# A three-layer graph attention kernel on one core: 806 columns instead of 808, and the node stage in four overlapped parts

## What is computed

```python
def _egat_layer(nf, ef, src, dst, W_ni, W_nj, W_fij, W_node, attn, bias):
    f_ni = nf @ W_ni
    f_nj = nf @ W_nj
    f_fij = ef @ W_fij
    f_out = f_ni[src] + f_nj[dst] + f_fij + bias
    f_out = jax.nn.leaky_relu(f_out, 0.2).reshape(-1, H, D)
    e = jnp.einsum('ehd,hd->eh', f_out, attn)
    emax = jax.ops.segment_max(e, dst, num_segments=N)
    a = jnp.exp(e - emax[dst])
    denom = jax.ops.segment_sum(a, dst, num_segments=N)
    a = a / denom[dst]
    h = (nf @ W_node).reshape(-1, H, D)
    m = h[src] * a[:, :, None]
    h_out = jax.ops.segment_sum(m, dst, num_segments=N)
    return (h_out, f_out)
...
h = jnp.maximum(_layernorm(x, axis=-1), 0.0)
for l in range(NL):
    nfh, efh = _egat_layer(nf, ef, src, dst, W_ni[l], W_nj[l], W_fij[l], W_node[l], attn[l], bias[l])
    nf = nfh.mean(axis=1)
    ef = efh.mean(axis=1)
return x + nf
```

## Time and profile before

| what | value |
|---|---|
| median of three runs | 3382.18 us |
| the profiled execution | 3382.53 us |
| its span, first to last instruction | 3380.7 us |
| PE busy | 2677.5 us, 79% |
| DVE busy | 2183.4 us, 65% |
| ACT busy | 1648.5 us, 49% |
| POOL busy | 2459.0 us, 73% |
| moved by DMA | 346.73 MB, mean 103 GB/s |

### The profile page before, as it was taken

The page is one execution under the profiler, slowest core; times in us unless marked ns, Lnnn a source line. Parts: engine busy times, 40 slices in busy tenths (PEclk is TensorE's granted clock), DMA queues, the critical chain, the costliest instruction groups (busy, mean ns, idle before and its releaser), DMA issues.

```text
span 3380.7 us, 34349 instructions
## 1 busy us (share of the span) xinstructions
PE 2677.5 (79%) x8858; PEld 1997.1 (59%) x8858; DVE 2183.4 (65%) x5325; ACT 1648.5 (49%) x3374; POOL 2459.0 (73%) x2595
## 2 busy tenths in 40 slices
PE   2299988888887288888888988827888888888883
PEld 1177766666665256666666666625666666666663
DVE  5288876767676247667676766624766767676663
ACT  0166655555555045555555555513555555555541
POOL 5777777777775777777777777667777777777773
PEclk8655555555555555555555555555555555555555
DMA  6143433333322323333323233232233232322222
GB/s 226 50 132 108 138 107 112 103 117 104 117 80 105 97 74 108 110 107 107 123 95 122 95 107 101 84 102 83 85 102 100 85 104 95 103 90 85 87 75 80
DMA packets 131212, 346.73 MB, mean 103 GB/s; under 512 B 48232, under 2 KB 88682, under 8 KB 111444
## 3 DMA queue, kind: packets, MB, share of 16 engines
q1 hardware_dynamic: 45492, 282.83, 22.3%
q0 software_dynamic: 82688, 46.77, 8.7%
q10 hardware_dynamic: 2838, 14.94, 1.1%
HBM read 131.12 MB, written 213.25 MB: 102 GB/s over the span
## 4 chain that ended last, share of the span: by engine, by line
POOL 51%; PE 19%; issue 18%; DMA 7%; DVE 4%; ACT 1%; POOLq 0%; DVEq 0%; ACTq 0%
POOL rows L453 49%; PE f_ps L567 7%; PE f_ps L575 7%; DMA rows<-nf_tab,src_sb 5%; PE xT_ps L557 4%; POOL edge_first L464 2%; DVE U L1070 1%; DMA U<-fix_tab 1%; POOL z L507 1%; DVE lr L1004 1%; DVE U L906 1%; PE wide_ps L639 1%; ACT f_low L686 0%; ACT up L731 0%; PE xT_ps L627 0%
## 5 line engine op out<-in xcount | busy, mean ns | idle before, releaser
L453 POOL DMA_INDIRECT rows<-nf_tab,src_sb x2424 | 2288.3, 944 | 761.6 <-issue 728.7
L575 PEld LDWEIGHTS f_ps<-w_out,lr 128*128 128x128 f32 x4848 | 1167.5, 331 | 622.4 <-issue 577.7
L567 PE MATMUL f_ps<-xT,w_edge 97*128 97x512 f32 x1212 | 1157.3, 1057 | 10.4 <-ACT xT L678 10.4
L557 PE MATMUL xT_ps<-ident,rows 128*97 128x128 f32 x2424 | 692.0, 439 | 502.2 <-DMA rows<-nf_tab,src_sb 352.1
L575 PE MATMUL f_ps<-w_out,lr 128*128 128x36 f32 (+1 forms) x4848 | 1052.8, 371 | 17.9 <-DVE lr L1004 17.8
L1004 DVE TENSOR_TENSOR lr<-f_ps,f_low 128x512 f32<-128x512 f32 x606 | 416.3, 687 | 890.5 <-ACT f_low L686 886.5
L557 PEld LDWEIGHTS xT_ps<-ident,rows 128*97 128x97 f32 x2424 | 518.2, 279 | 558.4 <-DMA rows<-nf_tab,src_sb 350.0
L1070 DVE TENSOR_TENSOR_SCAN U<-wide_ps,U 128x272 f32<-128x272 f32 (+1 forms) x1224 | 797.9, 715 | 1.2 <-ACT wide_ps L720 0.7
L678 ACT ACTIVATE xT<-xT_ps 97x512 f32<-97x512 f32 x606 | 357.7, 590 | 396.0 <-PE xT_ps L557 390.8
L686 ACT ACTIVATE f_low<-f_ps 128x512 f32<-128x512 f32 x606 | 360.6, 595 | 336.4 <-PE f_ps L567 334.7
L720 ACT ACTIVATE wide_ps<-e_dec 128x289 f32<-128x289 f32 (+1 forms) x612 | 403.4, 676 | 161.8 <-DVE U L1070 158.9
(11 more groups left out here) (135 smaller groups left out, 615.5 us busy)
## 6 DMA issues: line engine op xcount, KB each, us to landing
u_tab<-up SPq DMA_DIRECT2D x150, 1088.0 KB, 4.2
rows<-nf_tab,src_sb POOLq DMA_INDIRECT x2424, 2.4
first_st<-edge_first SPq DMA_DIRECT2D x48, 768.0 KB, 6.0
ef_tab<-ef_new SPq DMA_DIRECT2D x32, 768.0 KB, 4.2
ef_st<-ef_tab SPq DMA_DIRECT2D x32, 768.0 KB
edge_first<-first_st ACTq DMA_DIRECT2D x16, 768.0 KB, 12.1
ef_st<-in_edge_attr_dram SPq DMA_DIRECT2D x16, 672.0 KB
U<-fix_tab SPq DMA_DIRECT2D x3, 1062.5 KB
```

The costliest lines, as they stand in the source:

```text
L453: eng.indirect_dma_start(rows[q % RING][:, c * K:c * K + D], None, nf_tab[:, :], bass.IndirectOffsetOnAxis(ap=src_sb[:, t:t + 1], axis=0)) ...
L557: mm = eng.transpose(xT_ps[y][0:K, u * P:(u + 1) * P], rows3[q % RING][:, a * GT + u, :], ident[:, :])
L567: eng.matmul(f_ps[n % 3][:, :], w_edge[l][:, :], xT[y][0:K, :], start=True, stop=True).then_inc(f_ready, 1)
L575: mm = eng.matmul(f_ps[n % 3][:, u * m:(u + 1) * m], lr[y][:, u * P:(u + 1) * P], w_out[l][:, 0:m], start=True, stop=True)
```

## The change

T is computed as the number of columns that the edges need, 806, instead of whole groups of four, 808; the last group of a layer has two columns, and transposes, copies, leaky step and scores are as wide as the group. The wait for gathered rows counts the real columns. The last block has 6 columns, the last super block 38.

The nodes form four parts of 8, 8, 4 and 5 columns. Part a's result lies in a PSUM bank of its own: the two banks of `wide_ps`, `f_ps[0]` and `f_ps[1]`. DVE prepares a part (lines 1185 to 1198) and takes the result of the part ahead of it after that, in `take_nodes`. In the last layer `take_nodes` adds the result to x itself, and SP stores the output in four pieces. Each wait and index that depends on the parts follows.

```diff
--- before.py
+++ after.py
@@ -36,8 +36,8 @@
     C = D + 1
     K = C + 2 * D
     DST0, EF0 = C, C + D
-    NG = -(-E // (P * GT))
-    T = NG * GT
+    T = -(-E // P)
+    NG = -(-T // GT)
     NS = -(-T // SUP)
     NB = -(-T // SB)
     GB = SB // GT
@@ -58,6 +58,9 @@
 
     def sub_w(b):
         return min(SB, T - b * SB)
+
+    def grp_w(g):
+        return min(GT, T - g * GT)
 
     def groups_to(q):
         l, s = divmod(q, NS)
@@ -161,7 +164,7 @@
         wide_ps = ps("wide_ps", [P, 2 * GT * P])
         dbc = [wide_ps[:, y * GT * P:(y + 1) * GT * P] for y in range(2)]
         wts = dbc[0][:, (C - D // 2) * W1:(C - D // 2) * W1 + H * SB]
-        n_ps = wide_ps[0:NQ, 0:NCOL * D]
+        n_ps = [a[0:NQ, :] for a in (dbc[0], dbc[1], f_ps[0], f_ps[1])]
         runs_ps = ps("runs_ps", [P, GT * P])
         same_b = [runs_ps[:, s * SUP:(s + 1) * SUP] for s in range(2)]
         cut_b = [runs_ps[:, (2 + s) * SUP:(3 + s) * SUP] for s in range(2)]
@@ -246,7 +249,7 @@
         fix_clear = sem("fix_clear")
         fix_in = [sem(f"fix_in{a}") for a in range(2)]
         marked = sem("marked")
-        z_in = [sem(f"z_in{a}") for a in range(3)]
+        z_in = [sem(f"z_in{a}") for a in range(4)]
         nd = sem("nd")
         s_turned = sem("s_turned")
         sT_ready = sem("sT_ready")
@@ -254,14 +257,13 @@
         x_out = sem("x_out")
 
         groups = [range(g, min(g + GT, NCOL)) for g in range(0, NCOL, GT)]
-        parts = [range(0, 2), range(2, 4), range(4, len(groups))]
+        parts = [range(0, 2), range(2, 4), range(4, 5), range(5, len(groups))]
         part_cols = [range(groups[p[0]][0], groups[p[-1]][-1] + 1) for p in parts]
         col_part = [a for a, cols in enumerate(part_cols) for _ in cols]
         NPART = len(parts)
-        assert part_cols[2][0] * D == GT * P
         JS, NDS = 11, 4 * NPART
         fix_cols = [range(0, part_cols[2][0]), range(part_cols[2][0], NCOL)]
-        part_fix = [0, 0, 1]
+        part_fix = [0, 0, 1, 1]
         FIXW = SUP * D
         DB = NQ
         DSTEP = -(-D // (GS - 3))
@@ -278,8 +280,9 @@
         def ef_in_count(q):
             return 16 * sum(ef_loads(a) for a in range(q % 2, q + 1, 2))
 
-        def visits(q, a):
-            return sum((v % NS) * GS + a < NG for v in range(q % RING, q + 1, RING))
+        def rows_sem_to(q, a):
+            return 16 * sum(grp_w((v % NS) * GS + a) for v in range(q % RING, q + 1, RING)
+                            if (v % NS) * GS + a < NG)
 
         def carry_of(u, w):
             return u[:, 0:CH * (w + 1)].rearrange("p (c t h) -> p c t h", t=w + 1, h=H)
@@ -416,10 +419,12 @@
                         eng.wait_ge(nf_ready, (l + 2) * NPART)
                         store_nf()
 
-                eng.wait_ge(nf_ready, (L + 1) * NPART + 1)
-                eng.dma_start(out.rearrange("(q b) d -> q (b d)", b=NCOL), x_sb[:, :]
-                              ).then_inc(x_out, 16)
-                eng.wait_ge(x_out, 16)
+                for a, cols in enumerate(part_cols):
+                    c = slice(cols[0] * D, (cols[-1] + 1) * D)
+                    eng.wait_ge(nf_ready, L * NPART + (a + 1))
+                    eng.dma_start(out.rearrange("(q b) d -> q (b d)", b=NCOL)[:, c], x_sb[:, c]
+                                  ).then_inc(x_out, 16)
+                eng.wait_ge(x_out, 16 * NPART)
 
             @block.gpsimd
             def _(eng):
@@ -518,8 +523,8 @@
                                            u_end[:, :], None,
                                            bounds_check=N - 1, oob_is_err=False
                                            ).then_inc(u_fixed, 16)
-                    gather_z(1)
-                    gather_z(2)
+                    for a in range(1, NPART):
+                        gather_z(a)
 
             @block.tensor
             def _(eng):
@@ -548,12 +553,12 @@
                         if a == 0:
                             eng.wait_ge(dst_spread, (q + 1) * D)
                             eng.wait_ge(ef_put, q + 1)
-                        eng.wait_ge(src_rows[q % RING][a], visits(q, a) * 16 * GT)
+                        eng.wait_ge(src_rows[q % RING][a], rows_sem_to(q, a))
                         if n >= 2:
                             eng.wait_ge(xT_ready, n - 1)
                         else:
                             eng.wait_ge(counted, NCOL)
-                        for u in range(GT):
+                        for u in range(grp_w(g)):
                             mm = eng.transpose(xT_ps[y][0:K, u * P:(u + 1) * P],
                                                rows3[q % RING][:, a * GT + u, :], ident[:, :])
                         mm.then_inc(turned, 1)
@@ -564,14 +569,15 @@
                         if n >= 3:
                             eng.wait_ge(sc_ready, n - 2)
                             eng.wait_ge(ef_ready, min(n - 2, (L - 1) * NG))
-                        eng.matmul(f_ps[n % 3][:, :], w_edge[l][:, :], xT[y][0:K, :],
+                        eng.matmul(f_ps[n % 3][:, 0:grp_w(g) * P], w_edge[l][:, :],
+                                   xT[y][0:K, 0:grp_w(g) * P],
                                    start=True, stop=True).then_inc(f_ready, 1)
 
                     def scores(g):
                         n, y = n0 + g, (n0 + g) % 2
                         eng.wait_ge(lr_ready, n + 1)
                         m = M if l < L - 1 else H
-                        for u in range(GT):
+                        for u in range(grp_w(g)):
                             mm = eng.matmul(f_ps[n % 3][:, u * m:(u + 1) * m],
                                             lr[y][:, u * P:(u + 1) * P], w_out[l][:, 0:m],
                                             start=True, stop=True)
@@ -636,7 +642,8 @@
                             node_turn(n + 1)
                         eng.wait_ge(sT_ready, l * len(groups) + (n + 1))
                         for u, b in enumerate(groups[n]):
-                            mm = eng.matmul(n_ps[:, b * D:(b + 1) * D],
+                            a, c = col_part[b], b - part_cols[col_part[b]][0]
+                            mm = eng.matmul(n_ps[a][:, c * D:(c + 1) * D],
                                             xT[n % 2][:, u * DB:(u + 1) * DB],
                                             w_mean[:, l * D:(l + 1) * D],
                                             start=True, stop=True)
@@ -675,7 +682,8 @@
                         eng.wait_ge(turned, n + 1)
                         if n >= 2:
                             eng.wait_ge(f_ready, n - 1)
-                        eng.activation(xT[y][0:K, :], xT_ps[y][0:K, :], ACT.Copy
+                        w = grp_w(g) * P
+                        eng.activation(xT[y][0:K, 0:w], xT_ps[y][0:K, 0:w], ACT.Copy
                                        ).then_inc(xT_ready, 1)
 
                     def lower(g):
@@ -683,7 +691,8 @@
                         eng.wait_ge(f_ready, n + 1)
                         if n >= 2:
                             eng.wait_ge(lr_ready, n - 1)
-                        eng.activation(f_low[y], f_ps[n % 3][:, :], ACT.Copy, scale=SLOPE
+                        w = grp_w(g) * P
+                        eng.activation(f_low[y][:, 0:w], f_ps[n % 3][:, 0:w], ACT.Copy, scale=SLOPE
                                        ).then_inc(f_low_ready, 1)
 
                     def take_scores(g):
@@ -694,14 +703,15 @@
                         if i == 0 and k >= 2:
                             eng.wait_ge(prod_done, k - 1)
                         eng.wait_ge(o_ready, n + 1)
-                        o3 = f_ps[n % 3][:, 0:GT * m].rearrange("p (t m) -> p t m", m=m)
-                        eng.activation(sc3[k % 2][:, i * GT:(i + 1) * GT, :], o3[:, :, 0:H],
+                        w = grp_w(g)
+                        o3 = f_ps[n % 3][:, 0:w * m].rearrange("p (t m) -> p t m", m=m)
+                        eng.activation(sc3[k % 2][:, i * GT:i * GT + w, :], o3[:, :, 0:H],
                                        ACT.Copy).then_inc(sc_ready, 1)
                         if l < L - 1:
                             if a == 0 and q >= 2:
                                 eng.wait_ge(ef_out[q % 2], ef_stores_to(q - 2))
                             c = ((q % 2) * SUP + a * GT) * D
-                            eng.activation(ef_new[:, c:c + GT * D]
+                            eng.activation(ef_new[:, c:c + w * D]
                                            .rearrange("p (t d) -> p t d", d=D),
                                            o3[:, :, H:M], ACT.Copy).then_inc(ef_ready, 1)
 
@@ -1001,7 +1011,8 @@
                         eng.wait_ge(f_low_ready, n + 1)
                         if n >= 2:
                             eng.wait_ge(o_ready, n - 1)
-                        eng.tensor_tensor(lr[y], f_ps[n % 3][:, :], f_low[y], ALU.max
+                        w = grp_w(g) * P
+                        eng.tensor_tensor(lr[y][:, 0:w], f_ps[n % 3][:, 0:w], f_low[y][:, 0:w], ALU.max
```

(24 more changed lines are left out.)

## The result

The changed kernel takes 3362.67 us, the median of six runs from 3361.76 to 3363.67, beside 3382.21 us for the kernel before, the median of six as well (3381.65 to 3383.82): a ratio of 0.9942, interval 0.9929 to 0.9954, or 19.5 us less. The forecast was 3370.3 us, with a range from 3365.5 to 3374.8. The sign was right, and the gain is larger than forecast by 7.6 us and lies outside the range.

A forecast was written before the change was run, and what follows sets the result against it. GpSimd's row gathers were taken as the bound, with slack at each layer's end. Width 3.9, layer changes 0.6, node stage 6.8, store 0.5 and start-up 0.05 sum to 11.9 us: 3382.18 - 11.9 = 3370.3 us, range 3365.5 to 3374.8.

The forecast's parts named there:

- What bounds the kernel: GpSimd's row gathers, one every 1.248 us, set the pace; at a layer's end GpSimd is some 6 us ahead.
- a sign of its being wrong: At a layer's end, the last awaited gather landing, the hand-over at group 189, moves to another group.
- Width, 3.9 us: At each layer's end, 806 columns for 808 shorten the last group's and block's steps: 1.3 us a layer.
- Node stage of the last layer, 6.8 us: At the kernel's end: PE's idle 7.55 us gone, fourth part costs 1.8, shorter last addition gains 1.05.
- The cover: In the last layer, z and fix_tab land in time for DVE's earlier preparation; at worst z costs 0.4 us.
- rival (2): Last layer: z or fix_tab late for DVE, PE again waits about 3.6 to 3.9 us, 3374.1 us; chance 0.07.
- Output store, 0.5 us: At the kernel's end, the last of four stores holds 78 KB instead of 391: 0.5 us off 6.15.
- Changes of layer, 0.6 us: Between layers: GpSimd's wait falls by 0.55 us, part 1 stretches z gathers 0.3 more; net 0.3 a boundary.
- (1): At each layer's end the two saved gathers count: 2.5 us a layer instead of 1.3, 3366.7 us; chance 0.07.
- (3): At layer changes eight long DVE steps stretch GpSimd 6.2 us a boundary instead of 3.6: 3376.1 us; chance 0.05.
- (4): The hand-over's landing is near its worst in each layer: 3 x 4.4 = 13.2 us, 3383.5 us; chance 0.04.
- (5): New addresses lengthen the row gathers' interval; above 11 ns slower by over 0.2%, at 12 ns 3391 us; chance 0.03.

The follow-up runs named there:

- The single store: The changed kernel, but with the whole output stored by one transfer after the last part: 3366.5 us, 0.9953 of the kernel before.
- the cut one: The changed kernel, but with the output stored after the last part, cut by partitions into 112 and 13: 3363.11 us, 0.9942 of the kernel before.
- the cut load: The changed kernel with each load of fix_tab cut by partitions into 112 and 13: 3362.98 us, 0.9945 of the kernel before.

## Why the prediction was wrong, point by point

**What bounds the kernel** was read rightly: same interval of the gathers, GpSimd's last gather of layer 0 still far ahead of PE, and in layers 0 and 1 the same hand-over, group 189. In layer 2 the last awaited landing is that of group 191, which the prediction had named as a sign of its being wrong; what it is worth stands under the width.

**Width, 3.9 us.** Right: the kernel with the width alone gained 4.3. The end of layer 0 in the chain after, the rows that answer to the earlier trace rows:

```profile
1013.97 3.81 DMA rows<-nf_tab,src_sb
...
1093.07 1.96 ACT up L741
1095.50 1.84 DVE U L1081 x6
```

The six scans take 1.84 us instead of 2.26, the forecast's 0.41, and the gather of `u_end` comes 1.28 us sooner after the hand-over, the forecast's 1.3. In layer 2 some 0.9 us more was gained. There the kernel before waited for the landing of the hand-over's gather (group 189) for 4.78 us:

```profile
3230.38 4.78 DMA rows<-nf_tab,src_sb
```

The last such wait of the changed kernel is this one, eight gathers further on in the layer:

```profile
3233.38 2.36 DMA rows<-nf_tab,src_sb
```

The width alone had 2.32 us there and the parts alone, on 808 columns, 2.40. So it doesn't hang on the width; why it was late before isn't shown, and only one execution of the kernel before was profiled. The forecast had counted such an end in its range, at 0.8 us.

**Node stage of the last layer, 6.8 us.** The mechanism was right, and the sum small by 0.7: PE's stage is 6.3 us shorter (forecast 7.55 - 1.8 = 5.75), the last addition 1.2 (forecast 1.05). The fourth part cost 1.7 us; the rest is that each of the first two parts takes 0.2 less when the next follows at once. The cover held: DVE never waited for z or for `fix_tab` after its first step, so rival (2) didn't come about. Two experiments show how near it is: with the load 4.9 us sooner the z gathers are the bound, and with three parts DVE waits 2.95 us for z.

**Output store, 0.5 us: the first step that failed.** It gave 3.7. I priced 391 and 78 KB by the slope of u_tab's stores, (4.2 - 2.9) / 544 us per KB, and held against it that a landing has a fixed part. Those stores cover 128 partitions, the output 125, and the slope of the one isn't that of the other. The end of the span was 6.15 us away from a store of 391 KB, when 544 KB of `u_tab` landed in 2.9. That the smaller store took twice the time stood in the rows, and I took the whole 6.15 for an end that no store changes. It was 3.2 us of the 7.6 that the forecast missed. The single store (0.9953 of before where the changed kernel has 0.9942, some 3.8 us) and the cut one (3.4 less again on the same chip) show it.

**Changes of layer, 0.6 us: the second step that failed.** They gave 1.93 and 2.52 in the profiles, and 1.5 to 2.5 in the other kernels with four parts and uncut loads. The gap before the first scatter was forecast right (0.85 to 0.30; it became 0.41). The stretch of GpSimd was not: I counted long steps of DVE and moved them, at a price each of up to 0.78, and expected 0.3 more beside the z gathers. The price isn't one of the step but of the overlap at GpSimd's start: what is left of DVE's step, less some 0.15 us, which the earlier trace rows already allowed to be read. By parts, the steps cost 1.2, 0.9 and 1.5 us at the first change before. After, part 0 costs 1.45, part 1 0.64, and the four short steps nothing, as they fall between two starts. So the 1.5 us of the last part are the gain, and they were the term put at no change; part 1, forecast 0.3 dearer beside the z gathers, became 0.26 cheaper, because its copy starts while a long gather still runs, so that the next start comes only in the copy's last 0.15 us. That the steps would fall so stands nowhere in the forecast; it is luck of the order of work, and the cut load, which shifts them, takes part of it back. Three parts with the same overlap took 71.26 and 72.04 us, as before the change; that shows that the short last parts are what gained. This is 3.85 us of the miss; the little that is left lies in layer 2 and in the node stage.

**Rivals.** (1), the gathers count: refuted, six more a layer change nothing on a chip of the usual speed. (2), the overlap fails: not seen in the changed kernel, though with three parts instead of four it would have come about in part (PE waits 1.84 us). (3), the stretch grows with eight long steps: it fell instead, from six long instructions to three, and the rule on which it leaned works on starts, not on the number of steps. The Trainium skill (page "SBUF — State Buffer", section "SBUF: two separate sides") states an exclusive lock; the trace agrees in kind, for GpSimd alone. (4) and (5): neither the late landings nor a longer interval came; the interval is the same, 642 gathers in 800 us for 641.

With the store at 3.7 and the changes of layer at 4.45 the forecast's own sum would have been 11.9 + 3.2 + 3.85 = 18.95 us, 0.6 from the measured 19.5. The range was too narrow for one reason: for both terms I took bounds from rows of another kind, stores over 128 partitions for one over 125, and long steps for short ones.

## What to carry to other kernels

Price a transfer by rows with the same number of partitions; one over 125 partitions was worth cutting into 112 and 13 here, for a store and for a load. Where GpSimd issues gathers beside DVE, look at what DVE runs at the moment of each gather's start: a step that is over before the next start is free, one that catches a start costs what is left of it, less some 0.15 us, and one longer than the interval always catches one, though it can be in its last 0.15 us, as at 1131.68. Before making one input come sooner, look whether the other that the stage waits for is ahead by as much.

## What the runs showed of the hardware

- A store of 391 KB over 125 partitions (the single store beside the cut one): DMA share 0.28 to 0.32, 67 to 109 GB/s; over 112 and 13 partitions 0.91 and 278 GB/s. A load of 1062 KB over 125 partitions with one of 598 KB behind it: 12.3 us until DVE could start; cut in the same way 7.4.
- A GpSimd gather or scatter that starts during DVE's predicated copy or product of the node stage, steps with two operands in SBUF, ends 0.78 to 0.89 us after the step (26 of 26), alone it takes 0.94 to 0.98. One that started first keeps its length, and so does DVE's step. Where GpSimd starts only 0.01 to 0.04 us behind DVE (seven times in the experiments' kernels) it keeps its length and DVE's step gets up to 0.08 us longer; at 0.05 us behind it is held. DVE's product of the edge loop, 2.3 us with one operand in PSUM, holds no gather.
- The pace of the gathers differs a little between executions: from the first row gather of layer 1 to that of the hand-over, 760 columns on, 947.7 us in one profile of the changed kernel and 949.5 in another, which is of an execution 4.5 us slower than the median of its own chip.
